# Graph layer in two phases: the gathers of group 1 moved behind the rstd of two messages in GpSimd's order at the seam

## The chip, the cores and the metric

The kernel runs on one core of one Trainium2 chip. The metric is the device time of one execution in microseconds (us); lower is better. Three runs of the kernel before gave 1343.08, 1343.50 and 1343.95 us, median 1343.5 us.

## The reference, cut to what matters

12,500 nodes with 256 features each go through one layer of a graph network. What bears on the change:

```python
xn = layernorm(x)
# graph attention: rows of a table of all nodes, picked by index
xt = xn @ weight                                   # 12500 x 256, 4 heads of 64
alpha = softmax(leaky_relu(alpha_l[src] + alpha_r[dst]))
gnn = sum over heads of alpha * xt[dst[:n]]        # one gathered row per node
# linear attention over all nodes, then a two-layer network on it
msg = layernorm((Q (K^T V) / den) @ Wm)
mix = xn + layernorm(relu([xn, msg] @ W1) @ W2)
x = x + gnn + mix
# experts: a shared network, and the two best of four experts, gated
x = x + shared(layernorm(x)) + gated(layernorm(x))
```

The attention needs a sum over all 12,500 nodes (K^T V), and the gather needs the finished table of all nodes. So the work falls into two phases.

## The kernel before, in words

The nodes are cut into 25 groups of 512 (4 tiles of 128; the last group has 2 tiles). Phase 1 goes once over all groups: it normalizes x, writes the table `table_xt` (and the small table `table_al`) to HBM, and sums K^T V. Phase 2 goes over the groups again. Its steps overlap: one turn works on the message of group i, the network of group i-1 and the experts of group i-2. The steady turns run in a loop. Between the phases stands a seam written out by hand: `turn0` works on the message of group 0 and `turn1` on the message of group 1 and the network of group 0; then come `phase2(2, ..., second=True)` (on GpSimd `seam=True`), and the loop.

Every engine has its own instruction stream, and they meet in semaphores. Big matrix products are split into a high and a low part: TensorE (PE) does three products for each (`split_mm`, L255 to L257), ScalarE (ACT) makes the high part, VectorE (DVE) or GpSimd (POOL) subtracts to make the low part.

What the change and the prediction's steps touch, in the order in which it runs:

- GpSimd `gathers(par, tiles)` (L1812 to L1817): for each tile two indirect DMAs, one of 128 rows from `table_xt` into `xg` (L1814) and one from `table_al` into `ag` (L1816). Each raises the semaphore `gath0` or `gath1` by 16 when its data has landed. Eight of them make a group.
- GpSimd `rstd` (L1746 to L1757): waits for mean and variance (`mv_m` for the message), then four small instructions on 128x4 elements: `veps` (L1750), `nmean` (L1751), the power (L1753) and `nm` (L1757), which raises `rs_m`. It is what ScalarE's normalization waits for.
- TensorE: the denominators (L542), K^T V with Wv (L623, raises `kv_mm`), the first part of the hidden layer, the expansion of the denominators (L549, raises `dx`), the product with Wm (L630, raises `p1_pe`), the query of group 1, then the message of group 0 (`p2_m(0)`).
- VectorE: `kvT` (L1681, waits for `kv_mm`), `over_den(0)` (L1662, waits for `dx`), `g_lo` (L1685), `z_lo` (L1667), then the statistics of the message, which end in `mv_m` (L1195).
- ScalarE: `g_hi` (L968, waits for `p1_pe`), `z_hi` (L1151), and after `rs_m` the rows of the message `row_n` (L894), which TensorE transposes (L467).
- In `turn1` GpSimd makes the two low parts of the hidden layer h of group 0 (`h_lo`, L1820, each waits for a pair of `h_relu`), then the `rstd` of group 1's message, then that of y and that of z, then the first gathers of group 2.
- TensorE in `turn1`: after `p2_m(1)` it waits for both `h_lo` and does the products with W2; then `phase2(2)` begins with the transposes of group 1's `row_n`, which wait for `m_norm` tile by tile.
- VectorE waits for the whole of `gath1` only at the softmax of group 1 (L1351 in `soft_chain_in(1, 1, ...)`), at the end of its `turn1`. The sync queue (SP) waits for `gath1` at L439, then loads the indices of group 3 (L284), and behind that it loads x and the row statistics of group 2 (L443, L444).

A `pool.drain()` holds GpSimd's stream until what it has issued is done.

Of the kernel before, what the change touches and what calls it, by code (L numbers as in the profile page):

```python
# [59 lines left out]
def gps_layer(nc, A):  # L60

    ctx = ExitStack()
    with ctx:
# [3 lines left out]
        S = {name: ctx.enter_context(nc.semaphore("s_" + name)) for name in SEMAPHORES}  # L67
# [202 lines left out]
        def dma16(v, par):  # L270

            return 16 * (v // 2 + 1) if isinstance(v, int) else 8 * (v - par) + 16
# [1470 lines left out]
        def _(pool):  # L1743
            ptt, pts = pool.tensor_tensor, pool.tensor_scalar

            def rstd(which, mvs, count, done, plus_one=None):  # L1746

                if due(count):
                    pool.wait_ge(S[mvs], count)
                ptt(veps[which][:], mv[which][:, :, 1], eps[:], ALU.add)  # L1750
                pts(nmean[which][:], mv[which][:, :, 0], -1.0, None, ALU.mult)  # L1751
                pool.drain()
                ptt(rs[which][:], veps[which][:], neg_half[:], ALU.pow)  # L1753
                pool.drain()
                if plus_one is not None:
                    pts(plus_one, rs[which][:], 1.0, None, ALU.add)
                ptt(nm[which][:], nmean[which][:], rs[which][:], ALU.mult).then_inc(S[done], 1)  # L1757
# [54 lines left out]
            def gathers(par, tiles):  # L1812
                for j in tiles:
                    pool.indirect_dma_start(xg[par][:, j, :], None, table_xt.ap(), bass.IndirectOffsetOnAxis(  # L1814
                        idx[par][:, 1, j:j + 1], 0)).then_inc(S[f"gath{par}"], 16)
                    pool.indirect_dma_start(ag[par][:, j, :], None, table_al.ap(), bass.IndirectOffsetOnAxis(  # L1816
                        idx[par][:, 0, j:j + 1], 0)).then_inc(S[f"gath{par}"], 16)  # L1817

            def low(out, src, hi, done):
                ptt(out, src, hi, ALU.subtract).then_inc(S[done], 1)  # L1820
# [53 lines left out]
            def turn0():  # L1874
                pool.wait_ge(S["tables"], 1)
                pool.wait_ge(S["idx0"], 2 * dma16(0, 0))
                gathers(0, range(T))
                pool.wait_ge(S["idx1"], 2 * dma16(1, 1))
                gathers(1, (0, 1))
                pool.drain()  # L1880
                rstd(LM, "mv_m", 1, "rs_m")
                gathers(1, (2, 3))
                pool.drain()

            def turn1():
                for n in range(2):
                    pool.wait_ge(S["h_relu"], 2 * n + 2)
                    low(h_lo[:, 2 * n:2 * n + 2, :], relu[n][:], h_hi[:, 2 * n:2 * n + 2, :], "h_lo")
                pool.wait_ge(S["m_norm"], T)
                rstd(LM, "mv_m", 2, "rs_m")  # L1890
                rstd(LY, "mv_y", 1, "rs_y")
                rstd(LZ, "mv_z", 1, "rs_z")
                pool.wait_ge(S["gnn"], 1)
                pool.wait_ge(S["idx0"], 2 * dma16(2, 0))
                gathers(0, (0, 1))

            turn0()
            turn1()
            phase2(2, 0, seam=True)
            steps(pool, phase2, 3, NG - 1)  # L1900
# [26 lines left out]
```

## Time and profile before

| What | Value |
|---|---|
| Three runs | 1343.08, 1343.50, 1343.95 us |
| The profiled execution's own time | 1352.19 us |
| Its span in the profile | 1350.4 us |
| TensorE busy | 1312.1 us, 97% |
| VectorE busy | 1094.3 us, 81% |
| GpSimd busy | 762.7 us, 56% |
| ScalarE busy | 733.6 us, 54% |
| Mean granted clock of TensorE | 0.997 of full speed |

The profiled execution is 8.7 us longer than the median of the runs; durations and positions below are its own, in us from the start of its span. "Idle before" is the time in which an engine did nothing ahead of an instruction, and the name behind the arrow is what released it. "issue" says that the profile shows no releaser; "remote" says that a semaphore released it at a moment that fits the end of no instruction in the profile. The ends of TensorE's instructions are modelled.

### The profile page before, as it was taken

How to read it: one execution, taken by the hardware profiler on the slowest of the kernel's cores; microseconds unless marked ns; L12 is line 12 of the kernel's file. 1: busy time of each engine (PE TensorE's matmuls, PEld its weight loads, DVE VectorE, ACT ScalarE, POOL GpSimd, SP SyncE). 2: the span in 40 equal slices, each digit the busy share in tenths (PEclk: the TensorE clock that was granted, in tenths of full speed). 3: DMA queues.
4: the chain of work that ended last, by engine and by line, in shares of the span. 5: the costliest groups of instructions: out<-in, count | busy, mean ns of one | idle time of the engine just before them, and what ended most of it. 6: DMA issues, size and time to landing. Idle time of an engine off the chain costs nothing.

```text
span 1350.4 us, 26301 instructions
## 1 busy us (share of the span) xinstructions
PE 1312.1 (97%) x8812; PEld 1134.8 (84%) x8812; DVE 1094.3 (81%) x2597; ACT 733.6 (54%) x1332; POOL 762.7 (56%) x815
## 2 busy tenths in 40 slices
PE   6999999788999999999999999999999999999998
PEld 6999999676888888888888888888888888888886
DVE  6867677788888888888888888888888888888875
ACT  4555555344646555555646555555645555555654
POOL 5767766735455564656455564656455564656531
PEclk9999999999999999999999999999999999999999
DMA  6787767422121321222121221222121221222000
GB/s 211 250 275 244 245 208 249 135 56 72 35 70 56 78 70 32 68 65 76 36 68 55 78 70 32 68 65 77 36 68 55 78 70 32 70 64 68 26 17 22
DMA packets 65459, 123.23 MB, mean 91 GB/s; under 512 B 31725, under 2 KB 36176, under 8 KB 65422
## 3 DMA queue, kind: packets, MB, share of 16 engines
q1 hardware_dynamic: 57422, 109.25, 25.1%
q0 software_dynamic: 8000, 13.53, 4.6%
q8 instruction: 19, 0.31, 0.1%
q14 instruction: 18, 0.15, 0.0%
HBM read 70.41 MB, written 52.32 MB: 91 GB/s over the span
## 4 chain that ended last, share of the span: by engine, by line
PE 86%; DVE 4%; issue 3%; ACT 3%; POOL 1%; DVEq 1%; POOLq 1%; ACTq 1%
PE psum L255 25%; PE psum L257 25%; PE psum L256 25%; PE psum L467 5%; PE psum L659 1%; PE psum L708 1%; PE psum L699 1%; PE psum L650 1%; ACT scaleT L982 1%; ACTq L1077 1%; PE psum L718 1%; PE psum L542 1%; ACT relu L1075 1%; DVE gnn L1465 1%; POOL ag L1816 0%
## 5 line engine op out<-in xcount | busy, mean ns | idle before, releaser
L1820 POOL TENSOR_TENSOR h_lo<-relu,h_hi 128x1024 fp32r<-128x1024 f32 (+1 forms) x50 | 118.4, 2368 | 148.5 <-ACT h_hi L977 148.4
L255 PE MATMUL psum<-w_hi,h_hi 128*128 128x256 f32 x588 | 166.5, 283 | 1.0 <-ACT e L988 0.8
L257 PE MATMUL psum<-w_hi,h_lo 128*128 128x256 f32 x588 | 166.0, 282 | 0.0
L256 PE MATMUL psum<-w_lo,h_hi 128*128 128x256 f32 x588 | 165.4, 281 | 0.0
L1820 POOL TENSOR_TENSOR s_lo<-relu,s_hi 128x512 fp32r<-128x512 f32 (+1 forms) x45 | 82.7, 1838 | 121.4 <-ACT s_hi L1078 119.8
L255 PE MATMUL psum<-z_hi,w_hi 128*128 128x512 f32 (+1 forms) x300 | 121.6, 405 | 2.4 <-issue 1.1
L255 PE MATMUL psum<-xT_hi,w_hi 128*128 128x512 f32 (+1 forms) x300 | 119.6, 399 | 0.1
L1814 POOL DMA_INDIRECT xg<-table_xt,idx x100 | 99.3, 993 | 35.5 <-issue 31.6
L976 ACT ACTIVATE relu<-psum,h_bias 128x512 f32<-128x512 f32 (+1 forms) x100 | 67.9, 679 | 94.3 <-issue 81.0
L257 PE MATMUL psum<-xT_hi,w_lo 128*128 128x512 f32 (+1 forms) x300 | 117.2, 391 | 0.0
L257 PE MATMUL psum<-z_hi,w_lo 128*128 128x512 f32 (+1 forms) x300 | 117.0, 390 | 0.0
L256 PE MATMUL psum<-xT_lo,w_hi 128*128 128x512 f32 (+1 forms) x300 | 116.9, 390 | 0.0
L256 PE MATMUL psum<-z_lo,w_hi 128*128 128x512 f32 (+1 forms) x300 | 116.9, 390 | 0.0
L255 PEld LDWEIGHTS psum<-w_hi,h_hi 128*128 128x128 f32 x588 | 110.8, 188 | 2.7 <-ACT e L988 1.0
L1816 POOL DMA_INDIRECT ag<-table_al,idx x100 | 94.9, 949 | 30.5 <-issue 30.5
L256 PEld LDWEIGHTS psum<-w_lo,h_hi 128*128 128x128 f32 x588 | 110.9, 189 | 1.1
L257 PEld LDWEIGHTS psum<-w_hi,h_lo 128*128 128x128 f32 x588 | 110.7, 188 | 0.0
L894 ACT ACTIVATE row_n<-psum,nm_m,rs_m 128x256 f32<-128x256 f32 x98 | 47.4, 563 | 101.8 <-POOL nm_m L1757 101.8
L1449 DVE SCALAR_TENSOR_TENSOR base<-xb,rn,b_bc 128x256 f32<-128x256 f32 x98 | 92.1, 980 | 0.2 <-issue 0.2
L988 ACT ACTIVATE e<-psum,e_bias 128x512 f32<-128x512 f32 (+1 forms) x100 | 67.3, 676 | 38.4 <-PE psum L257 38.0
L1790 POOL TENSOR_TENSOR k_lo<-kf,k_hi 128x1024 fp32r<-128x1024 f32 x25 | 62.9, 2518 | 39.5 <-DVE k_hi L1232 39.5
L255 PE MATMUL psum<-mT_hi,w_hi 128*128 128x512 f32 (+1 forms) x200 | 80.8, 404 | 0.7 <-DVE mT_lo L1598 0.7
(274 smaller groups left out, 4291.6 us busy)
## 6 DMA issues: line engine op xcount, KB each, us to landing
xb<-in_x SPq DMA_DIRECT2D x47, 448.0 KB, 3.8
xT_hi_table<-x1T_hi SPq DMA_DIRECT2D x25, 512.0 KB, 2.8
xT_lo_table<-x1T_lo SPq DMA_DIRECT2D x25, 512.0 KB, 3.6
xT_hi<-xT_hi_table SPq DMA_DIRECT2D x25, 512.0 KB
xT_lo<-xT_lo_table SPq DMA_DIRECT2D x25, 512.0 KB
table_xt<-xts SPq DMA_DIRECT2D x24, 455.0 KB, 3.0
out<-xmid SPq DMA_DIRECT2D x24, 448.0 KB
xb<-in_x SPq DMA_DIRECT2D x47, 64.0 KB, 3.8
```

The costliest lines, as they stand in the source:

```text
L255: pe.matmul(out, wh, xh, start=first, stop=False)
L256: pe.matmul(out, wh, xl, start=False, stop=False)
L257: return pe.matmul(out, wl, xh, start=False, stop=last)
L467: last = pe.transpose(psum[:, b + c, j * R:(j + 1) * R], src[:, j, c * P:(c + 1) * P], ident[0:R, 0:R])
L894: act.activation(out[:, j, :], src(j), ACT.Identity, bias=nm[which][:, j:j + 1], scale=rs[which][:, j:j + 1]).then_inc(S[done], 1)
L976: act.activation(out[:, 0:t * R], colT(b, t=t), ACT.Relu, bias=bias)
L988: act.activation(e1[:, e, 0:t * R], colT(bank, t=t), ACT.Relu, bias=e1_bias[:, e:e + 1]).then_inc(S["e1_relu"], 1)
L1449: last = stt(base[:, j, :], xb[par][:, j, :], rn2[par][:, 0, j:j + 1], b2_bc[:], ALU.mult, ALU.add)
L1790: ptt(k_lo[par][:], kf[par][:], k_hi[par][:], ALU.subtract).then_inc(S["k_split"], 1)
L1814: pool.indirect_dma_start(xg[par][:, j, :], None, table_xt.ap(), bass.IndirectOffsetOnAxis(idx[par][:, 1, j:j + 1], 0)).then_inc(S[f"gath{ ...
L1816: pool.indirect_dma_start(ag[par][:, j, :], None, table_al.ap(), bass.IndirectOffsetOnAxis(idx[par][:, 0, j:j + 1], 0)).then_inc(S[f"gath{ ...
L1820: ptt(out, src, hi, ALU.subtract).then_inc(S[done], 1)
```

## The change

In `turn0` the gathers of group 1's tiles 0 and 1 move from ahead of the drain and the `rstd` of group 0's message to behind that `rstd`, together with the wait for their indices. Tiles 0, 1 and 2 are gathered there. The gathers of tile 3 move into `turn1`, behind the two low parts of h and ahead of the `rstd` of group 1's message, with a drain of their own.

```diff
--- before.py
+++ after.py
@@ -1875,17 +1875,18 @@
                 pool.wait_ge(S["tables"], 1)
                 pool.wait_ge(S["idx0"], 2 * dma16(0, 0))
                 gathers(0, range(T))
-                pool.wait_ge(S["idx1"], 2 * dma16(1, 1))
-                gathers(1, (0, 1))
                 pool.drain()
                 rstd(LM, "mv_m", 1, "rs_m")
-                gathers(1, (2, 3))
+                pool.wait_ge(S["idx1"], 2 * dma16(1, 1))
+                gathers(1, (0, 1, 2))
                 pool.drain()
 
             def turn1():
                 for n in range(2):
                     pool.wait_ge(S["h_relu"], 2 * n + 2)
                     low(h_lo[:, 2 * n:2 * n + 2, :], relu[n][:], h_hi[:, 2 * n:2 * n + 2, :], "h_lo")
+                gathers(1, (3,))
+                pool.drain()
                 pool.wait_ge(S["m_norm"], T)
                 rstd(LM, "mv_m", 2, "rs_m")
                 rstd(LY, "mv_y", 1, "rs_y")
```

## Rows read from the trace of the kernel before

**Rows 1.** The page: busy time of the engines.
```profile
PE 1312.1 (97%) x8812; PEld 1134.8 (84%) x8812; DVE 1094.3 (81%) x2597; ACT 733.6 (54%) x1332; POOL 762.7 (56%) x815
```

**Rows 2.** Busy time by stretch of the seam: start:end, length, each engine, granted clock, DMA.
```profile
263.00:268.00 5.00, 1.86 (x7) 1.33 (x8) 1.92 (x7) 0.00 (x0) 3.78 (x4) 1.00 0.33 55
...
310.00:318.00 8.00, 4.95 (x19) 3.25 (x18) 6.55 (x19) 6.56 (x11) 5.57 (x8) 0.88 0.17 31
...
340.00:355.00 15.00, 15.00 (x100) 12.65 (x100) 12.83 (x35) 7.17 (x13) 6.85 (x13) 1.00 0.01 3
```

**Rows 3.** Instructions of GpSimd in order of time, up to the first rstd: start, duration.
```profile
261.77 0.94 POOL L1816 DMA_INDIRECT ag<-table_al,idx  x1 [0.30 <-issue]
263.01 0.95 POOL L1814 DMA_INDIRECT xg<-table_xt,idx  x1 [0.30 <-issue]
...
266.76 0.94 POOL L1816 DMA_INDIRECT ag<-table_al,idx  x1 [0.30 <-issue]
277.53 0.20 POOL L1750 TENSOR_TENSOR veps_m<-mv_m,eps 128x4 f32<-128x4 f32 x1 [9.83 <-DVE mv_m L1195]
...
279.25 0.20 POOL L1757 TENSOR_TENSOR nm_m<-nmean_m,rs_m 128x4 f32<-128x4 f32 x1
```

**Rows 4.** The three engines between the denominators and the message of group 0.
```profile
259.54 2.05 PE L623 MATMUL psum<-w_raw,wv 128*128 128x128 f32 x8
...
264.60 0.73 PE L549 MATMUL psum<-rdenT,den_sel 128*128 128x512 f32 x2 [1.61 <-DVE rdenT L1433]
...
266.32 0.49 DVE L1681 TENSOR_TENSOR kvT<-psum,head_mask 128x128 f32<-128x128 f32 x2 [1.78 <-remote]
...
266.87 1.13 PE L630 MATMUL psum<-wm,kvT 128*128 128x256 f32 x4 [1.54 <-issue]
...
269.87 1.29 DVE L1662 TENSOR_TENSOR qf<-qf,psum 128x512 f32<-128x512 f32 x2 [3.06 <-remote]
...
269.97 0.60 ACT L968 ACTIVATE g_hi<-psum 128x512 fp32r<-128x512 f32 x1 [11.75 <-remote]
...
273.11 0.36 PE L255 MATMUL psum<-g_hi,z_hi 128*128 128x256 f32 x1 [2.31 <-DVE z_lo L1667]
```

**Rows 5.** GpSimd behind the first rstd, up to the second.
```profile
279.93 1.09 POOL L1814 DMA_INDIRECT xg<-table_xt,idx  x1 [0.47 <-issue]
...
283.82 0.95 POOL L1816 DMA_INDIRECT ag<-table_al,idx  x1 [0.30 <-issue]
288.88 2.40 POOL L1820 TENSOR_TENSOR h_lo<-relu,h_hi 128x1024 fp32r<-128x1024 f32 x1 [4.11 <-ACT h_hi L977]
293.29 2.78 POOL L1820 TENSOR_TENSOR h_lo<-relu,h_hi 128x1024 fp32r<-128x1024 f32 x1 [2.01 <-ACT h_hi L977]
297.81 0.28 POOL L1750 TENSOR_TENSOR veps_m<-mv_m,eps 128x4 f32<-128x4 f32 x1 [1.73 <-DVE mv_m L1195]
...
299.89 0.20 POOL L1757 TENSOR_TENSOR nm_m<-nmean_m,rs_m 128x4 f32<-128x4 f32 x1
```

**Rows 6.** The sync queue: its load behind `gath1`.
```profile
286.44 0.33 SPq L284 DMA_DIRECT2D idx<-in_src  x1
```

**Rows 7.** Rows and transposes of the message of group 1.
```profile
300.12 1.93 ACT L894 ACTIVATE row_n<-psum,nm_m,rs_m 128x256 f32<-128x256 f32 x4 [6.91 <-POOL nm_m L1757]
...
301.94 1.04 PE L467 MATMUL psum<-ident,row_n 128*128 128x128 f32 x8
302.74 0.48 PE L255 MATMUL psum<-xT_hi,w_hi 128*128 128x512 f32 x1
```

**Rows 8.** VectorE and GpSimd reading at the same time, and VectorE's addition at 300.
```profile
300.14 1.23 DVE L1711 TENSOR_TENSOR base<-base,gnn 128x1024 f32<-128x1024 f32 x1
...
346.77 1.26 DVE L1542 TENSOR_TENSOR h_lo<-relu,h_hi 128x512 fp32r<-128x512 f32 x2
...
347.46 0.67 POOL L1751 TENSOR_SCALAR nmean_m<-mv_m 128x4 f32<-128x4 f32 x1
```

**Rows 9.** TensorE's transposes of z in the first full turn, with the wait ahead.
```profile
314.24 1.91 PE L467 MATMUL psum<-ident,row_z 128*128 128x128 f32 x8 [2.89 <-ACT row_z L894]
```

## The prediction

> **What bounds the kernel now.** The page comes first: TensorE is busy for 97% of the span [rows 1]. In the loop nothing that GpSimd does can gain anything, so the change lives where TensorE is not full. The busy time by stretch shows where that is. Between 263 and 268 TensorE works 1.86 of 5 us, between 310 and 318 it works 4.95 of 8, and from 340 on it has no hole at all [rows 2]. So the seam is a chain of waits, and whatever it loses or gains stays: behind it stand full turns that can take nothing back. The change touches this seam once, not once for each of the 25 groups.
>
> The instructions in order of time then say what the chain waits for. The first rstd on GpSimd begins at 277.53 after 9.83 us of idleness that VectorE's `mv_m` ended, while the last gather ahead of it was over at 266.76 + 0.94 = 267.70 [rows 3]. So the gathers as instructions did not hold the rstd. That is the first thing to see: by GpSimd's own order the first half of the edit gains nothing. The second thing is less plain. Three waits ahead of message 0 end later than their releasers in the code. `kvT` waits for L623, which ended at 259.54 + 2.05 = 261.59, and begins only at 266.32, after VectorE stood idle for 1.78. `g_hi` waits for L630, over at 266.87 + 1.13 = 268.00, and begins at 269.97, 1.97 later. `qf` waits for L549, over at 265.33, and begins at 269.87 [rows 4]. All three are marked "remote", all lie in or just behind the time of group 1's early gathers, and all stand on the chain kvT, L630, `g_hi`, `z_lo`, message 0 at 273.11 [rows 4].
>
> **The change part by part.**
>
> *Gathers of tiles 0 and 1 out of the stretch ahead of the rstd.* Four indirect DMAs go, 263.01 to 267.70 [rows 3], and the drain now follows group 0's last gather, which ended at 262.71. By instruction order: gain 0, since the rstd waits for `mv_m` [rows 3]. If the three late releases come from those gathers or the drain behind them, the gain is 1.78 at `kvT` plus 1.97 at `g_hi`, 3.75 in sum, for these two stand one behind the other; the 3.06 at `qf` runs beside the second and is not added [rows 4]. So this part is bounded by 0 and 3.75. I take 0, and the other end is the first rival: the transfers have no instruction in common with TensorE's releases, and the execution with the profile took 1352.19 against a median of 1343.5, so waits that fit no instruction may be the profiled run's own.
>
> The Trainium skill (SBUF — State Buffer, section "Who interferes with whom") says that a DMA never contends with a compute engine, and that only VectorE and GpSimd share a port. By it those waits can't come from the gathers' data, and this part gains nothing, as I have taken it; the late starts of `g_hi` and `qf` beside a finished releaser are the trace's word against it [rows 4].
>
> *Three tiles behind the first rstd instead of two.* Two more DMAs. The four took from 279.93 to 283.82 + 0.95 = 284.77, so one costs 0.95 plus the 0.30 gap [rows 5], and six end at 284.77 + 2.5 = 287.3. The first `h_lo` begins at 288.88, released by ScalarE [rows 5]. Only the drain lies between. What a drain behind a gather costs no row of these views shows. Below it is 0. Nearest above it is the landing: the sync queue, which waits for all of `gath1`, issued its load at 286.44 [rows 6], 1.67 behind the last gather. I take 1.7, as the drain's purpose is to wait for what was issued: 287.3 + 1.7 = 289.0 against 288.88, so the first `h_lo` slips by 0.1 to 0.5. It ends near 291.5, and the second begins at 293.29 by ScalarE's release [rows 5], with 1.8 to spare. TensorE needs both low parts at once, so nothing is lost. Cost 0; the cover is the 2 us between the two low parts.
>
> *The wait for group 1's indices* moves along; they are as old as before, so it costs 0.
>
> *Tile 3 between the second low part and the second rstd.* This is the price. The second `h_lo` ends at 293.29 + 2.78 = 296.07. Two gathers with a short start take 2.4, to 298.4. The drain with 1.7 ends at 300.1. Before, the rstd began at 297.81, when `mv_m` came, and its last instruction ended at 299.89 + 0.20 = 300.09 [rows 5]. In the first rstd the time from the start of `veps` to the end of `nm` was 279.45 - 277.53 = 1.92 [rows 3]. So alone it would end at 302.1, 2.0 later. But it meets VectorE's addition on `base` at 300.14, 1.23 long, with both inputs in SBUF [rows 8]. A small GpSimd instruction beside such a pair took 0.67 us at 347.46 and ended just when VectorE's pair did [rows 8], where `veps` of the same 128x4 form took 0.20 alone [rows 3]. If `veps` waits for the addition's end at 301.37, then 1.72 more give 303.1, 3.0 later. If the drain cost 0, the rstd would begin at 298.5 and end near 300.4, 0.3 late.
>
> What of that reaches TensorE? The rows of message 1 ran from 300.12 for 1.93, to 302.05, and TensorE, busy with W2 until 301.94, took the eight transposes in 1.04 without a gap and went on at 302.74 [rows 7]. With the rstd 3.0 later the rows end at 305.1; the last tile's two transposes are a quarter of the 1.04, so TensorE goes on at 305.3, 2.6 later. With 2.0 it is 1.6; with 0.3 nothing. I take 2.5: the drain waits for the landing and the port is taken. What follows (the high part of message 1, its low part, the query of group 2, the network's second layer norm, z) is released by these transposes, so it moves as a block, and no hole is closed by it: the 2.89 us wait for z at 314.24 [rows 9] hangs on the same chain.
>
> The same section of the Trainium skill says that a VectorE instruction with two SBUF inputs contends with a GpSimd instruction that reads SBUF. The pair at 346.77 agrees; without the rule, 1.6 would stand in place of 2.6.
>
> *What else hangs on `gath1`.* It is complete near 300.1 instead of 286.4. VectorE asks for it at the end of its turn, after 310 in this trace. The sync queue's loads behind it (indices of group 3, x and statistics of group 2) slip from 286.4 and 299 to 300 or 301, and x of group 2 is read in the loop's first turns, past 350. Cost 0.
>
> **The sum:** 0 + 0 + 2.5 = +2.5 us on the profiled execution's 1352.19. It is a stall in the seam, so I add it unchanged to the median: 1343.5 + 2.5 = **1346.0 us**, 0.19% more. About 0.2%, 2.7 us, is what a measurement of this kernel can tell from no change.
>
> **The rivals.**
>
> *1. The late releases were the gathers' doing (30%).* For it: they cluster under the gathers and end when the last transfers must be landing (last gather 267.70 plus 1.67 is 269.4, `qf` and `g_hi` begin at 269.87 and 269.97). Against it: the four gathers after the first rstd (279.93 to 284.77) have no such effect on the chain beside them. Gain 3.75, less 2.5: -1.2, so 1342.3 us; with the cheaper drain or port 1341.4. If only one of the two waits goes, 1344.1 to 1344.2.
>
> *2. TensorE's clock falls once more (22%).* The granted clock was 0.88 between 310 and 318, a stretch at the lower level (1.2 of 2.4 GHz) behind a wait of 2.89 us and eight transposes that came one by one with their rows [rows 2, 9]. The new hole at 302 has the same shape, some 2 us of wait and eight transposes fed by the rows. If it is long enough, multiplications that are the chain run at half speed for a while: 0.12 of 8 us at 310 to 318 is 1 us of cycles lost there, and it went on past 318, so 1 to 1.7 more. That gives 1343.5 + 2.5 + 1.5 = 1347.5 us, **slower**. It decides from the point where the wait ahead of the transposes gets near 2.9; mine is 1.8 to 3.
>
> *3. The drain doesn't wait for the data, or the second rstd is hidden (10%).* Then tile 3 costs 0.3 at GpSimd and nothing at TensorE, the change does nothing, and the time is 1343.5.
>
> The forecast itself, cost between 1.6 and 2.9 with nothing gained, has 38%.
>
> **How the numbers follow.** The range takes in rival 1 with its cheaper drain below (1341.4) and rival 2 above, 1347.8: from 1341.3 to 1347.8. The forecast's own range is 1345.1 to 1346.6. Faster by over 0.2% needs less than 1340.8: only rival 1 with more gained than the two waits, 0.07. Slower needs more than 1346.2: nearly all of rival 2 and a quarter of the forecast's case, 0.31. Within it is the rest, 0.62.
>
> **What the changed profile would show.** Right: the second rstd's `veps` begins at 300 or later after two gathers, relative to the second `h_lo`'s end 4 us instead of 1.7; `row_n` of message 1 starts some 3 us later against TensorE's W2; ahead of the transposes TensorE waits about 1.8 us for `row_n`, where it had no wait; the first `h_lo` moves by under 0.5. The first rstd follows `mv_m` as before. The forecast is wrong if the idle time ahead of `kvT`, `qf` and `g_hi` shrinks and message 0 begins near 269.4 instead of 273.11 in runs without the profile too (rival 1), if a stretch of lower clock appears behind 305 (rival 2), or if TensorE meets the transposes without a wait (rival 3).

## The result and the profile after

| Compared, eleven runs each | Value |
|---|---|
| Before, median | 1344.13 us (1343.08 to 1347.0) |
| After, median | 1349.74 us (1345.73 to 1351.06) |
| Ratio, with its 95% interval | 1.0035 [1.0024, 1.0046] |
| The profiled execution of after, its own time | 1350.36 us |
| Its span | 1348.5 us |

The change makes the kernel slower by 0.35%. The prediction was 1346.0 us with a range up to 1347.8, so the result lies above the range. A second comparison, in a later group (chip C), gave 1.0045 [1.003, 1.006]. Chips differ by more than the change does (the kernel before took 1343.7, 1344.1, 1344.8 and 1350.5 us on four of them), so everything below goes by ratios to the kernel before on the same chip. Which chip the first comparison ran on is not on record.

The page of the changed kernel, its line of busy times, answers to [rows 1]:

```profile
PE 1315.5 (98%) x8812; PEld 1138.6 (84%) x8812; DVE 1099.7 (82%) x2597; ACT 734.4 (54%) x1332; POOL 764.8 (57%) x815
```

TensorE has the same 8812 instructions and is busy 3.4 us longer. Equal work that takes longer is the first sign that not only waits were added. The busy time by stretch of the changed kernel (columns as in [rows 2]) says where:

```profile
263.00:268.00 5.00, 5.00 (x20) 4.05 (x19) 3.17 (x7) 1.75 (x3) 0.00 (x0) 0.84 0.06 8
...
296.00:303.00 7.00, 5.03 (x32) 3.88 (x31) 3.39 (x10) 2.84 (x5) 4.01 (x8) 0.94 0.27 76
303.00:310.00 7.00, 7.00 (x27) 5.61 (x26) 6.58 (x15) 0.12 (x1) 0.56 (x3) 0.81 0.00 0
...
328.00:340.00 12.00, 9.36 (x56) 8.67 (x55) 9.77 (x34) 2.23 (x5) 4.32 (x4) 0.86 0.51 156
```

From 263 to 268 TensorE is full, where it worked 1.86 us before [rows 2]: the late releases are gone. But from 296 to 303 it now has a hole, and in the next 7 us it is full at a granted clock of 0.81. GpSimd of the changed kernel, in order of time (start, duration):

```profile
261.74 0.94 POOL L1816 DMA_INDIRECT ag<-table_al,idx  x1 [0.30 <-issue]
273.04 0.20 POOL L1750 TENSOR_TENSOR veps_m<-mv_m,eps 128x4 f32<-128x4 f32 x1 [10.36 <-DVE mv_m L1195]
...
281.83 0.94 POOL L1816 DMA_INDIRECT ag<-table_al,idx  x1 [0.30 <-issue]
285.94 5.72 POOL L1820 TENSOR_TENSOR h_lo<-relu,h_hi 128x1024 fp32r<-128x1024 f32 x2 [3.16 <-issue]
291.81 2.03 POOL L1814 DMA_INDIRECT xg<-table_xt,idx  x1
294.14 0.95 POOL L1816 DMA_INDIRECT ag<-table_al,idx  x1 [0.30 <-issue]
296.89 0.20 POOL L1750 TENSOR_TENSOR veps_m<-mv_m,eps 128x4 f32<-128x4 f32 x1 [1.80 <-issue]
...
297.45 1.80 POOL L1753 TENSOR_TENSOR rs_m<-veps_m,neg_half 128x4 f32<-128x4 f32 x1 [0.16 <-issue]
299.40 0.20 POOL L1757 TENSOR_TENSOR nm_m<-nmean_m,rs_m 128x4 f32<-128x4 f32 x1 [0.15 <-issue]
```

Two things stand here against [rows 5]. The two low parts of h are one block of 5.72 us; they were 2.40 and 2.78 with a gap. And tile 3's gathers with their drain lie ahead of the second `veps_m`, released by nothing ("issue" behind a gather is the drain). The other engines of the changed kernel at the same two places:

```profile
262.88 0.49 DVE L1681 TENSOR_TENSOR kvT<-psum,head_mask 128x128 f32<-128x128 f32 x2
265.80 0.60 ACT L968 ACTIVATE g_hi<-psum 128x512 fp32r<-128x512 f32 x1 [7.61 <-PE psum L630]
...
289.33 3.68 DVE L1303 TENSOR_TENSOR w_lo<-w_raw,w_hi 128x1280 fp32r<-128x1280 f32 x1
...
299.63 1.93 ACT L894 ACTIVATE row_n<-psum,nm_m,rs_m 128x256 f32<-128x256 f32 x4 [10.86 <-POOL nm_m L1757]
...
300.25 1.80 PE L467 MATMUL psum<-ident,row_n 128*128 128x128 f32 x8 [1.92 <-ACT row_n L894]
301.81 0.48 PE L255 MATMUL psum<-xT_hi,w_hi 128*128 128x512 f32 x1
...
302.49 0.63 PE L257 MATMUL psum<-xT_hi,w_lo 128*128 128x512 f32 x1
...
305.77 0.39 PE L256 MATMUL psum<-xT_lo,w_hi 128*128 128x512 f32 x1
```

The transposes wait 1.92 us for `row_n`, where [rows 7] had no wait, and the multiplications behind them take 0.63 us each until 305.5, where the same ones take 0.39 afterwards: the lower of the two clock levels.

**A ruler for all profiles.** The edit touches the time between the first `veps_m` and the transposes of `row_n` for the message of group 2, the third set of them in phase 2 (the expectations below call them group 4's). For each profile I cut the span there. Before the edit, first profile: 277.53, 75.46 between the two, 997.41 behind. The other cuts are in this table; the starts are rows like the ones shown.

| Kernel (chip) | First `veps_m` | From there to group 2's transposes | Behind |
|---|---|---|---|
| before, third profile (C) | 271.88 | 75.51 | 992.91 |
| before, fourth (D) | 271.81 | 75.79 | 993.90 |
| before, again (A) | 271.70 | 80.10 | 993.70 |
| after | 273.04 | 82.37 | 993.09 |
| after, again (C) | 271.65 | 84.00 | 992.95 |

Behind the seam nothing changes, as the prediction said. The 8.7 us by which the first profile of the kernel before stood above its median are not in every execution: 277.53 against 271.9 is the late releases, and its last part is 4 us longer as well. This is the third profile of the kernel before, unedited, at the places of [rows 4, 5]; then its row of group 2's transposes and the one of the changed kernel's profile:

```profile
262.48 0.49 DVE L1681 TENSOR_TENSOR kvT<-psum,head_mask 128x128 f32<-128x128 f32 x2
...
271.88 0.20 POOL L1750 TENSOR_TENSOR veps_m<-mv_m,eps 128x4 f32<-128x4 f32 x1 [3.76 <-DVE mv_m L1195]
...
283.24 2.41 POOL L1820 TENSOR_TENSOR h_lo<-relu,h_hi 128x1024 fp32r<-128x1024 f32 x1 [4.12 <-ACT h_hi L977]
287.66 2.80 POOL L1820 TENSOR_TENSOR h_lo<-relu,h_hi 128x1024 fp32r<-128x1024 f32 x1 [2.01 <-ACT h_hi L977]
292.15 0.28 POOL L1750 TENSOR_TENSOR veps_m<-mv_m,eps 128x4 f32<-128x4 f32 x1 [1.68 <-DVE mv_m L1195]
...
347.39 1.03 PE L467 MATMUL psum<-ident,row_n 128*128 128x128 f32 x8
```

```profile
355.41 1.03 PE L467 MATMUL psum<-ident,row_n 128*128 128x128 f32 x8
```

The trace also gives the clock stretch by stretch. The falls to the lower level at the seam last 3.4 us, or twice that, and cost half their length: 1.7 us for each 3.4. In the middle part the four profiles of the kernel before have 1 (first), 1 (third), 2 (fourth) and 4 (again) such stretches of 3.4 us; the two of the changed kernel have 3 and 4. With 1.7 us taken off for each, the middle part is 72.4 to 73.8 us before and 77.2 to 77.3 after, some 3.9 us more. So the clock explains why profiles of one kernel differ, and only a part of the loss.

### The profile page after: what moved, and what is told of

It reads as the page before. It is cut to its first block, busy times and chain, and to the rows that moved or that the text cites. A ratio compares the mean times of both kernels' runs of the same rounds, so it can differ in the third digit from the quotient of the medians.

```text
span 1348.5 us, 26302 instructions
## 1 busy us (share of the span) xinstructions
PE 1315.5 (98%) x8812; PEld 1138.6 (84%) x8812; DVE 1099.7 (82%) x2597; ACT 734.4 (54%) x1332; POOL 764.8 (57%) x815
## 4 chain that ended last, share of the span: by engine, by line
PE 88%; DVE 4%; issue 3%; ACT 2%; POOL 1%; POOLq 1%; DVEq 1%; ACTq 0%
PE psum L255 25%; PE psum L257 25%; PE psum L256 25%; PE psum L467 5%; PE psum L659 3%; PE psum L708 1%; PE psum L650 1%; PE psum L718 1%; PE psum L549 1%; PE psum L542 1%; DVE gnn L1465 1%; POOLq L1754 0%; POOL xg L1814 0%; POOL h_lo L1820 0%; POOL ag L1816 0%
```

## The experiments

Theory A: the loss is in the order of the work, at two places, the drain ahead of the low parts and tile 3 ahead of the second rstd. Its rivals: the late releases decide it, or TensorE's clock does. Fifteen runs were made, in four groups on chips A, B, C and D.

### The kernel before, unedited, three times

> The kernel before, unchanged, for a second profile and for the noise. The profile on record has three late releases ahead of message 0 (kvT, qf, g_hi, 3.75 us on the chain) that the changed kernel's profile does not have, and its execution was 8 us longer than the runs. Theory A, the late releases belong to that one execution: here kvT begins within 0.2 us of rdenT's end, the first rstd begins near 273 instead of 277.5, and the profiled execution's time is within 2 us of the median. Theory B, they belong to the early gathers of group 1: kvT waits about 1.8 us again and the first rstd begins near 277.5. Ratio 1.000 by both.

Ratio 1.0005 [0.9994, 1.0016], and no late release: `kvT` at 262.40, first `veps_m` at 271.70. So the three waits of [rows 4] are not part of every execution. But its middle part is 80.10, 4.3 to 4.6 longer than in the two profiles below, with the same code and order. What differs is the clock, and TensorE's wait for `e`, which is 0.9 to 1.2 us longer: the mean clock is 0.993 of full speed there and 0.997 in the others. Some eighty runs of the kernel before on chips A, C and D show the same: those with a mean clock of 0.997 average 1342.1 to 1342.5 us by chip, those with 0.993 average 1346.7 to 1347.0. The difference of 0.004 is 5.4 us of full-speed work in 1343; the times differ by 4.6. (The expected 2 us between the profiled execution and the median were missed: it took 1347.34, 2.3 above the median of its group and 3.3 above the kernel before's.)

> The kernel before once more, unedited, for its profile on this chip. Theory A: kvT near 262.5 us, first rstd near 271.5 to 273, no late release. Theory B: the late releases depend on the chip or the execution; they appear here (kvT near 266, qf near 269.8, first rstd near 277) if the comparison of the changed kernel on this chip comes out near or under 1.000, and are absent if it comes out above 1.002.

First `veps_m` at 271.88, no late release, and the comparison in that group came out at 1.0045: as both theories allow.

> The kernel before, unedited, for its profile on this chip. Theory A (the late releases belong to the chip): first rstd at 276 us or later together with a loop 2 us or more longer than on the chip of the third group (907 us from group 4's transposes to the last group's), or near 272 together with a loop of 907 us. Theory B (they belong to the single execution): first rstd and loop length go their own ways.

First `veps_m` at 271.81 and 993.90 behind the seam. (From group 2's transposes to those of the last full group it is 906.9 to 907.8 us in all profiles of chips A, C and D, 909.2 to 909.4 in the three of chip B, and 911.4 in the first profile.) Where late releases appear the loop is longer too, so a property of the chip or its memory has a part in them. Whether the edit has one as well is the question of a section below.

### One half of the change at a time

`first_half`: all of group 1 behind the first rstd, nothing behind the low parts.

```diff
-                pool.wait_ge(S["idx1"], 2 * dma16(1, 1))
-                gathers(1, (0, 1))
                 pool.drain()
                 rstd(LM, "mv_m", 1, "rs_m")
-                gathers(1, (2, 3))
+                pool.wait_ge(S["idx1"], 2 * dma16(1, 1))
+                gathers(1, (0, 1, 2, 3))
                 pool.drain()
```

> All four tiles of group 1 gathered behind the first rstd, nothing put into turn1. Theory 1 (the cost sits at tile 3 ahead of the second rstd: wait for row_n and a stretch of lower clock behind it): 1344 us, ratio 0.999 to 1.001, TensorE meets the transposes of message 1 without a wait. Theory 2 (the first half costs as well: the drain behind six or eight gathers outlasts ScalarE's release of the first low part): the drain ends 2.5 us later still than in the changed kernel, both h_lo are late, TensorE waits for them ahead of W2, 2 to 4 us, 1346 to 1350 us.

Measured 1.0013 [1.0003, 1.0022] on chip A. The drain pushed the first low part to 285.97, both ran as one block of 5.67, and TensorE waited for them:

```profile
291.68 0.39 PE L255 MATMUL psum<-w_hi,h_hi 128*128 128x256 f32 x1 [1.28 <-POOL h_lo L1820]
```

So the part that was costed at 0 costs about 0.13%, 1.7 us, with four tiles there rather than three; this is its second theory, at the lower end.

`second_half`: tiles 0 and 1 stay early, only tile 3 and a drain go behind the low parts.

```diff
-                gathers(1, (2, 3))
+                gathers(1, (2,))
                 pool.drain()
...
                     low(h_lo[:, 2 * n:2 * n + 2, :], relu[n][:], h_hi[:, 2 * n:2 * n + 2, :], "h_lo")
+                gathers(1, (3,))
+                pool.drain()
```

> Tiles 0 and 1 ahead of the first rstd as before, tile 2 behind it, tile 3 with its drain behind the two low parts of h as in the changed kernel. Theory 1: the whole loss is here: 1348.5 to 1350 us, ratio 1.0035 to 1.0045, TensorE waits about 2 us for row_n of message 1 and then runs 3.4 us at the lower clock. Theory 2: part of it, 1345.5 to 1347.5, since the low parts come on time and the second h_lo ends earlier against mv_m.

Measured 1.0029 [1.0016, 1.0041]. The low parts stand apart again, and this is the price of tile 3 alone:

```profile
288.53 2.80 POOL L1820 TENSOR_TENSOR h_lo<-relu,h_hi 128x1024 fp32r<-128x1024 f32 x1 [2.02 <-ACT h_hi L977]
...
292.75 0.94 POOL L1816 DMA_INDIRECT ag<-table_al,idx  x1 [0.30 <-issue]
295.52 1.14 POOL L1750 TENSOR_TENSOR veps_m<-mv_m,eps 128x4 f32<-128x4 f32 x1 [1.83 <-issue]
...
298.24 0.20 POOL L1757 TENSOR_TENSOR nm_m<-nmean_m,rs_m 128x4 f32<-128x4 f32 x1 [0.15 <-issue]
```

```profile
299.09 1.80 PE L467 MATMUL psum<-ident,row_n 128*128 128x128 f32 x8 [1.73 <-ACT row_n L894]
300.65 0.48 PE L255 MATMUL psum<-xT_hi,w_hi 128*128 128x512 f32 x1
300.97 0.39 PE L256 MATMUL psum<-xT_lo,w_hi 128*128 128x512 f32 x1
```

From the first `veps_m` to the second `nm_m` it is 25.48 us (298.24 - 272.76), where [rows 3, 5] had 22.36 (299.89 - 277.53): 3.1 later, against 3.0 forecast. The drain took 1.83 against 1.7. TensorE waits 1.73 us and goes on at 300.65, 27.89 behind the first `veps_m`; in the third profile of before it goes on 25.22 behind it. That is 2.7 later, against 2.6 forecast. One part of its first theory failed: the multiplications behind this wait run at the full clock (0.39 each), so the same hole was not followed by a slow stretch here. The two halves sum to 0.42%, the whole change measured 0.35 and 0.45%: within their intervals of about 0.1 each way the halves add up, and tile 3 is about two thirds.

### The drains alone

`no_t3_drain`: the changed kernel without the drain behind tile 3's gathers.

```diff
                 gathers(1, (3,))
-                pool.drain()
```

> The changed kernel without the drain behind tile 3's gathers. Theory 1: the second rstd begins 1.8 to 2 us earlier, TensorE's wait for row_n is under 0.5 us, no stretch of lower clock follows it: 1344 to 1346 us. Theory 2: the late low parts stay, so at least half of the loss stays: 1347 to 1349 us.

Measured 1.0028 [1.0018, 1.0038] on chip A, 1348.5 us: its second theory, the loss stays for the most part. It is 0.07%, 0.9 us, under the first comparison of the whole change, about half of the drain's 1.8, though the intervals overlap. `no_drains` shows where the rest may go: there the drain behind the first rstd goes too (chip D).

```diff
                 gathers(1, (0, 1, 2))
-                pool.drain()
...
                 gathers(1, (3,))
-                pool.drain()
```

> The changed kernel with the gathers where it has them and both added or kept drains taken out (behind the first rstd and behind tile 3's gathers). Theory A (the drain that holds the low parts is what makes tile 3's place costly: without it the low parts end near 290.5 us, and tile 3's two gathers fit into the 3.3 us in which GpSimd then waits for mv_m): second rstd at most 1 us later than without them, no wait of TensorE for row_n at the transposes beyond 0.5 us, ratio to the kernel before 1.000 to 1.002. Theory B (the place itself costs, drain or not): second rstd 2 to 3 us later, TensorE waits over 1 us there, ratio 1.0025 or more.

```profile
292.94 0.94 POOL L1816 DMA_INDIRECT ag<-table_al,idx  x1 [0.30 <-issue]
293.89 0.41 POOL L1750 TENSOR_TENSOR veps_m<-mv_m,eps 128x4 f32<-128x4 f32 x1
294.27 0.46 POOL L1751 TENSOR_SCALAR nmean_m<-mv_m 128x4 f32<-128x4 f32 x1
295.89 1.81 POOL L1753 TENSOR_TENSOR rs_m<-veps_m,neg_half 128x4 f32<-128x4 f32 x1 [1.16 <-issue]
```

Ratio 1.0018 [1.0008, 1.0027], TensorE waits 1.17 us for `row_n`: the ratio is theory A's, the wait is theory B's. The low parts are free again (2.42 and 2.78 us, apart), and `veps_m` starts right behind the gather. But L1753 stands 1.16 us behind "issue": `rstd` has a drain of its own between `nmean` and the power, and that one now waits for the gathers. From `veps_m` to the end of `nm_m` it is 4.16 us where the third profile of before has 2.27 (292.15 to 294.22 + 0.20). A drain that is deleted behind a gather is paid, at least in part, at the next drain. (The power's own 1.81 us is not part of that: it took 1.80 in the changed kernel too, with its drain in place.)

### The order without either cost

`first_half_no_drain`: all four tiles behind the first rstd, no drain behind them.

```diff
-                gathers(1, (2, 3))
-                pool.drain()
+                pool.wait_ge(S["idx1"], 2 * dma16(1, 1))
+                gathers(1, (0, 1, 2, 3))
```

> All four tiles of group 1 behind the first rstd, and no drain behind them. In the run with the drain the first h_lo began at 285.97, 14.5 us behind the first rstd's start, held by the drain alone; undisturbed it stands 11.35 behind. Theory D (the drain is the first half's cost): the first h_lo begins about 12.5 behind the rstd, when the eighth gather is over, VectorE's z_lo and w_lo of that time are no longer than before, TensorE's wait of 1.28 us ahead of W2 goes, ratio 0.9995 to 1.0005. Rival (the mass of gathers itself costs, or the clock): the ratio stays near 1.0013.

`t3_behind_y`: the changed kernel, but tile 3 behind the rstd of y and without its drain.

```diff
-                gathers(1, (3,))
-                pool.drain()
                 pool.wait_ge(S["m_norm"], T)
                 rstd(LM, "mv_m", 2, "rs_m")
                 rstd(LY, "mv_y", 1, "rs_y")
+                gathers(1, (3,))
```

> The changed kernel with tile 3's gathers behind the rstd of y instead of ahead of the rstd of message 1, and without their drain; GpSimd is idle there for about 5 us. Theory P (the place ahead of the rstd is the second half's cost, whether drained or not): row_n of message 1 comes as before, TensorE meets its transposes without a wait, and what stays is the first half's 0.0013 or less: ratio 1.0005 to 1.0015. Rival (splitting group 1 costs wherever tile 3 stands, through gath1 or the late loads of the sync queue): 1.0025 or more.

Both ran on chip B, where before took 1350.5 us: 0.9993 [0.9984, 1.0002] and 0.9982 [0.9973, 0.9991]. No wait at message 1's transposes in either, though TensorE still waits 1.3 us for `h_lo` in `t3_behind_y`, whose drain stayed. Neither theory had foreseen a ratio under 1 for it (1.0005 or more). `t3_behind_y` is the only kernel of the study that is measurably faster than the one before it, and only on that chip. Why only there is taken up below.

`behind_no_drain` puts the two together (tiles 0 to 2 behind the first rstd without a drain, tile 3 behind the rstd of y), on chip C beside the changed kernel itself.

> The changed kernel with both of its costs taken out: tiles 0 to 2 behind the first rstd but without the drain behind them, tile 3's gathers behind rstd y and without a drain. Theory A (these two places are the loss): the low parts of h start as soon as relu is there and apart from one another (near 2.4 us each instead of 5.7), no wait of TensorE for h_lo nor for row_n at the transposes; ratio to the kernel before 0.997 to 1.0005, and 0.3 to 0.5% under the changed kernel in the same group. Theory B (the loss is in stretches of lower TensorE clock that any shift of this seam brings): ratio 1.002 or more all the same, with 10 to 14 us at the lower level as in the changed kernel.

> The changed kernel once more, unedited, on the chip of this group. Theory A (the loss belongs to the order of the work: tile 3's gathers delay the second rstd, the drain behind the first holds the low parts of h): ratio 1.002 to 1.005, with the second rstd of message 3 us or more later behind the first than in the kernel before, and TensorE waiting 1.5 to 2 us for row_n at the transposes. Theory B (how much of it shows depends on how many late releases the kernel before has in its seam): ratio 0.999 to 1.002 wherever the kernel before shows kvT, qf and g_hi released late ahead of the first rstd (kvT after 266 us, first rstd after 276 us), and 1.002 to 1.005 where it does not.

The changed kernel 1.0045 [1.003, 1.006], this one 1.0008 [0.9998, 1.0018]; by the medians, 1344.95 against 1350.2, it is 0.39% ahead of the changed kernel. The waits of TensorE from 290 to 345, first of the changed kernel's first profile, then of this one (us in total, times, longest):

```profile
PE psum L467 <- ACT row_z L894: 2.9, 1, 2.9
PE psum L255 <- ACT e L988: 2.6, 1, 2.6
PE psum L467 <- ACT row_n L894: 1.9, 1, 1.9
```

```profile
PE psum L467 <- ACT row_z L894: 2.9, 1, 2.9
PE psum L255 <- ACT e L988: 2.1, 1, 2.1
```

The wait for `row_n` is gone, and nearly the whole loss with it. Theory A holds; the rival that any shift of the seam brings slow stretches would have given 1.002 or more. The second profile of the changed kernel shows its other cost at its largest, VectorE's work beside the six gathers, and then GpSimd's low parts:

```profile
280.47 2.77 DVE L1465 SCALAR_TENSOR_TENSOR gnn<-xg,soft_e,gnn 128x64 f32<-128x64 f32 x12
...
286.04 1.49 DVE L1303 TENSOR_TENSOR w_lo<-w_raw,w_hi 128x1280 fp32r<-128x1280 f32 x1
...
288.04 4.72 POOL L1820 TENSOR_TENSOR h_lo<-relu,h_hi 128x1024 fp32r<-128x1024 f32 x2 [6.64 <-ACT h_hi L977]
```

The last of the six gathers ended at 281.39. The low parts wait 6.64 us more, and the name behind the arrow misleads: both run without a pause, so both inputs were there by then, and the trace's record of the drain ends at 287.9, 0.4 behind VectorE's `w_lo`. TensorE then waited 0.95 us for `h_lo`.

What the drain waits for can be read from the packets of the gathers' DMA queue in the traces. All 31 drains that stand behind gathers at the seam (those inside `rstd` left out) ended 0.4 to 1.2 us behind the last packet of these gathers, the long ones too. So a long drain is late data. Where the third tile is gathered behind the first rstd, its packets meet two things: the sync queue's load of `xT_hi` and `xT_lo` (512 KB each), and VectorE's chain of `gnn`. In the changed kernel's first profile the DMA moved 378 GB/s while they waited (columns as in [rows 2]):

```profile
277.00:282.00 5.00, 5.00 (x23) 4.08 (x24) 4.23 (x14) 1.40 (x3) 3.78 (x5) 1.00 0.50 78
282.00:284.30 2.30, 2.30 (x12) 1.85 (x11) 2.15 (x11) 2.17 (x4) 0.78 (x1) 1.00 0.96 378
```

The packets of the first two tiles began 0.4 us behind the start of their second gather, those of the third 2.5 us behind it, at 284.4. In the second profile they trickled from 280.9 to 287.1. In the kernel before, the four gathers behind the rstd had sent nearly all of their packets when the load began (285.9, first profile). Which of the two held the third tile back, load or `gnn`, no run separates.

`behind_second` is `behind_no_drain` again, on chip D:

> The order without the drain behind the first rstd and with tile 3's gathers behind rstd y, once more, on the chip of this group. Theory A (the gain of the move is the absence of the late releases, so it is there only where the kernel before has them): ratio 0.996 to 0.999 on a chip where before_fourth shows a first rstd at 276 us or later, 1.000 to 1.002 where it is near 272. Theory B (no such dependence): 1.000 to 1.002 on every chip.

1.0005 [0.9996, 1.0015], beside a profile of before without late releases. That agrees with both theories; there is no second comparison on chip B, so whether this order is ahead there stays open.

### The late releases

`all_early` doubles the suspect: all eight gathers of group 1 in front of the first rstd, none behind it.

```diff
-                gathers(1, (0, 1))
+                gathers(1, (0, 1, 2, 3))
                 pool.drain()
                 rstd(LM, "mv_m", 1, "rs_m")
-                gathers(1, (2, 3))
-                pool.drain()
```

> The suspected cause doubled: all four tiles of group 1 are gathered ahead of the first rstd, in front of the one drain that is left, and none behind. Theory A (the late releases ahead of message 0 are the doing of group 1's early gathers, eight in a row behind group 0's): late releases of kvT, qf or g_hi appear in this profile whatever the chip, first rstd at 277 us or later; ratio 1.001 to 1.005. Theory B (they have nothing to do with group 1's gathers): kvT near 262.5; the drain ends 2.5 to 4 us later than in the kernel before (near 274) and sets the first rstd at 274 to 276; the low parts of h then meet a free GpSimd and start as soon as relu is there; ratio 0.999 to 1.002.

```profile
263.05 0.49 DVE L1681 TENSOR_TENSOR kvT<-psum,head_mask 128x128 f32<-128x128 f32 x2
...
272.32 0.94 POOL L1816 DMA_INDIRECT ag<-table_al,idx  x1 [0.30 <-issue]
275.61 0.20 POOL L1750 TENSOR_TENSOR veps_m<-mv_m,eps 128x4 f32<-128x4 f32 x1 [2.35 <-issue]
...
278.19 2.06 PE L467 MATMUL psum<-ident,row_n 128*128 128x128 f32 x8 [4.47 <-ACT row_n L894]
```

No late release under eight early gathers; `kvT` begins at 263.05. What the early gathers do cost is GpSimd's own order: the drain ends at 275.5 and the message waits 4.47 us for its rows (0.86 otherwise). Ratio 1.0033 [1.0019, 1.0046]. The profile is theory B's, the ratio is above its bound: it had left out that an rstd at 275.6 reaches TensorE in full. So early gathers alone are not enough to make the releases late, on chip C.

On chip B it looks different. There the two kernels that gather group 1 behind the rstd have one late release themselves, and it is one that the prediction did not list: VectorE's first step on the denominators (L1425), released by L542. First the profile on record, then `t3_behind_y`:

```profile
261.34 0.30 DVE L1425 TENSOR_SCALAR psum<-psum 128x128 f32<-128x128 f32 x1 [2.32 <-remote]
```

```profile
261.37 0.30 DVE L1425 TENSOR_SCALAR psum<-psum 128x128 f32<-128x128 f32 x1 [2.25 <-remote]
264.60 0.49 DVE L1681 TENSOR_TENSOR kvT<-psum,head_mask 128x128 f32<-128x128 f32 x2
```

In the third profile of before this step begins at 259.25, after 0.21. It is late ahead of group 1's first gather (263.01), so these gathers did not cause it. But the three releases behind it are late only in the two profiles that have group 1's gathers early as well, the one on record and `low_first` (chip B, next section). On chip B the first `veps_m` begins at 277.33 with them and at 273.42 and 273.55 without: 3.8 to 3.9 us, what rival 1 of the prediction gave (3.75). It is one profile against two, and the five other profiles with early gathers, on chips A, C and D, have no late release. So both may be needed, the chip's state and the early gathers. `t3_behind_y`'s 0.9982 fits that in part; its mean clock was also 0.001 higher than before's, worth 1.6 of its 2.4 us. The changed kernel itself was not run on chip B.

The Trainium skill (SBUF — State Buffer, "Who interferes with whom") says a DMA never contends with a compute engine. `all_early` agrees with it; the profiles of chip B show late semaphore releases, and no run shows what makes them late.

### The stall that both kernels have

`low_first` and `behind_low_first` put the first low part of group 1's h ahead of group 2's gathers, in the kernel before and in `behind_no_drain`.

```diff
-                    for n in range(2):
+                    for n in range(1 if seam else 0, 2):
...
                 rstd(LZ, "mv_z", 1, "rs_z")
+                pool.wait_ge(S["h_relu"], 6)
+                low(h_lo[:, 0:2, :], relu[0][:], h_hi[:, 0:2, :], "h_lo")
```

> The kernel before with one move of its own kind: in the seam GpSimd makes the first low part of group 1's h ahead of group 2's eight gathers, not behind them. Before, both low parts ran back to back at 318.5 to 323.3 (second profile of the kernel before) and one of VectorE's weighted sums of 64 columns stood still for all of them; TensorE then waited 3.0 us for e. Theory L (GpSimd's two low parts hold VectorE's second read and so TensorE): the weighted sums take about 3.4 us instead of 7.9, the wait for e goes, one stretch of lower clock behind it too: 1338 to 1341.5 us, ratio 0.9955 to 0.998. Rival (the wait for e is made up of something else, or the wait moves to the next stage): 0.999 to 1.000.

> behind_second with one more step: the first low part of group 1's h ahead of group 2's gathers in the seam, so that the long chain of gnn on VectorE is not held beside two low parts back to back. Theory A: the chain of gnn takes 2.8 us instead of 7.9, TensorE's wait for e (2.1 us) shrinks to under 1 us, ratio to the kernel before 0.9985 to 1.0005 where that has no late release. Theory B (e hangs on ACT's s part and the second low part, which now comes later, not on gnn): the wait for e stays at 2 us or more, ratio as behind_second or above.

1.0001 [0.9992, 1.001] and 1.0002 [0.9993, 1.0011]. The chain of `gnn` fell from 7.9 to 2.77 us in both, and TensorE's wait for `e` stayed at 2.6 and 2.1: the wait doesn't hang on `gnn`. `low_first`, on chip B, is the second profile with late releases, which look like those of [rows 4] (its L1425 is late too, by 2.26):

```profile
266.17 0.49 DVE L1681 TENSOR_TENSOR kvT<-psum,head_mask 128x128 f32<-128x128 f32 x2 [1.76 <-remote]
269.68 1.28 DVE L1662 TENSOR_TENSOR qf<-qf,psum 128x512 f32<-128x512 f32 x2 [3.02 <-remote]
```

## Why the prediction was wrong, step by step

- **Where the change acts** was right: the part of the span behind the seam is 993 us with and without it.
- **Early gathers out, gain 0** was right on chips A, C and D, where the first `veps_m` begins at 271.5 to 273.0 with either order: the rstd waits for `mv_m`, and the late releases belong to some executions. On chip B the profiles lean to rival 1, so there it is open. Two readings were off: the trace held a fourth late release (L1425, 2.32 us), ahead of group 1's gathers, which spoke against them as the only cause; and the price of all four was 5.6 us at the first rstd, not 3.75.
- **Tile 3 ahead of the second rstd, +2.5** was right in mechanism and in size: 3.1 us against 3.0 at GpSimd, 2.7 against 2.6 where TensorE goes on. In time `second_half` measured 0.29% [0.16, 0.41], 2.2 to 5.5 us, which does not contradict 2.5.
- **"Cost 0; the cover is the 2 us between the two low parts"** is the step that failed. With four tiles this half puts TensorE's going on behind message 1's transposes 1.5 us later (26.77 behind the first `veps_m` against 25.22) and measured 0.13% [0.03, 0.22], 1.7 us. In the changed kernel TensorE goes on 3.6 us later (28.77 against 25.22, and 30.42 against 26.83 in the two profiles that had one slow stretch on the way): 2.7 are tile 3's, so 0.9 is this half's. The term that was mis-sized is the drain, 1.7 us taken from a place behind four gathers. Behind six it held for 3.1 and 6.5 us in the two profiles of the changed kernel, the first low part slipped by 1.5 and 3.5 us where 0.1 to 0.5 was forecast, and the gap between the low parts was gone. I did not ask what the third tile's transfer would meet. That VectorE's `z_lo` and `w_lo` took 3.51 and 3.68 in the profile after, against 2.10 and 1.48 in the third profile of before, is no proof of a cost: `before_again` has 3.10 and 3.69 without any edit.
- **The sum** also left out the clock, as rival 2's business. Rival 2 named the right place: in both profiles of the changed kernel a slow stretch stands behind the new hole, eight multiplications at steps of 0.43 us instead of 0.23. But `second_half` has the hole without it, and the kernel before has such stretches at other places. What more of them the change brings is small on average: the mean clock of the eleven runs is 0.0003 lower than that of the kernel before on chip A (its runs in the first comparison have none on record), and 0.0013 lower in the comparison on chip C: 0.4 and 1.7 us. At an equal clock the loss is still there: runs of the changed kernel at 0.993 and 0.997 averaged 1350.7 and 1346.0 us, those of the kernel before 1346.7 to 1347.0 and 1342.1 to 1342.5, a difference of 3.5 to 3.9. That two of its runs took the forecast's 1346 is chance, not a hit: they are its fastest, at the higher clock.
- By terms: 2.7 (tile 3) and 0.9 (first half) make 3.6 at TensorE, with 0.4 to 1.7 for the clock 4.0 to 5.3; measured are 4.7 and 6.0 us, with intervals of 1.5 to 2 us each way. The split between clock and waits is by means of runs; no run took the clock's part away alone.
- **The chances.** Rival 2 had 22%. Its time (1347.5) was the nearest of the four, but it had only a part of the reason: what the first half costs stood in no rival.

## What to carry to other kernels

A group of gathers moved behind a critical instruction is free only if the next things on that queue have room for the gathers, the drain and what the drain will meet; here the free place was one instruction further on, behind the rstd of y, and it cost nothing there. A drain behind gathers costs what their data need at that place, so ask which other transfers run then. When a wait of some microseconds is put in front of a TensorE that was full, a stretch at half speed may follow it, 1.7 us here, in some kernels and not in others; compare runs at the same mean clock before giving it a share of the loss. And before costing anything on a wait marked "remote", take a second profile of the same kernel: three more of these had 5.6 to 5.8 us less in front of the seam.

## What the runs showed of the hardware that was not expected

- Identical code took from 1342.3 to 1347.2 us on one chip, and the mean granted clock of the run (0.997 or 0.993) tells which end it is at.
- A GpSimd drain behind indirect gathers ended 1.65 to 2.25 us behind the last gather in 27 of the 31 cases at the seam, but 3.1, 3.1, 6.5 and 6.7 us behind it in four, all of them behind six gathers in a row. In all 31 it ended 0.4 to 1.2 us behind the gathers' last packet.
- Ten profiles gather a third tile behind the first rstd. In seven its packets began within 0.25 us of the start of the last step of VectorE's `gnn` chain, and 0.3 to 0.8 us ahead of the end of the sync queue's load; in three they trickled, and the load lasted 5.1 to 5.3 us instead of 3.4 to 3.8. That VectorE holds up the writing of descriptors is one reading, that the load takes the DMA engines is the other; no run took either away.
- 12 short `gnn` steps on VectorE took 7.9 us beside two low parts on GpSimd, and 2.77 when these stood elsewhere (`low_first`, `behind_low_first`). The Trainium skill (SBUF — State Buffer, "Who interferes with whom") says that a VectorE instruction with two SBUF inputs contends with a GpSimd instruction that reads SBUF; the traces agree.
